# When VectorE's sequencer loads the register offsets of the chunk sums in a graph-network kernel

## The reference, cut to what matters

```python
# x [12500, 64], edge_attr_64 [400000, 64], src random, dst sorted (denser at low nodes)
msg = node_feat[src] + edge_feat
agg = jax.ops.segment_sum(msg, dst, num_segments=node_feat.shape[0])
h = jax.nn.relu(agg @ W1 + b1)
x = _layernorm(x + (h @ W2 + b2), axis=-1)
```

## Time and profile before

| | |
|---|---|
| median of three runs | 1650.94 us |
| profiled execution | 1655.22 us, span 1653.4 us |
| main stage | about 75 to 1550 us |
| busy: DVE, PE, POOL, ACT | 84%, 81%, 71%, 54% of the span |
| loads at line 898 | 125 |
| adds at line 906, marks at line 885, slots | 625, 313, 734 |

### The profile page before, as it was taken

One profiled execution on the slowest core, in us unless ns is written; L12 is line 12 of the kernel. 1 busy time (PEld: TensorE's weight loads), 2 busy tenths in 40 slices (PEclk: granted clock), 3 DMA queues, 4 the chain that ended last, 5 costly groups with the idle time before them and its releaser, 6 DMA issues. The chain is left out here.

```text
span 1653.4 us, 46879 instructions
## 1 busy us (share of the span) xinstructions
PE 1343.8 (81%) x18386; PEld 1195.7 (72%) x18387; DVE 1390.4 (84%) x2969; ACT 892.8 (54%) x1167; POOL 1169.7 (71%) x822
## 2 busy tenths in 40 slices
PE   1266777878888898888989899899988999899884
PEld 1255666767787787788878888788878887778653
DVE  5499999999988989999879898788889998788343
ACT  3734323335554554555566666566666667666352
POOL 5777888888777778778668777678677776857032
PEclk8557989999998998998999999899999999999885
DMA  6735444444444444444444444344444444433033
GB/s 178 144 82 111 104 95 106 105 104 101 102 95 91 105 89 95 101 108 90 90 97 89 96 91 92 84 86 93 97 87 90 96 91 85 83 65 69 14 70 73
DMA packets 229761, 154.81 MB, mean 94 GB/s; under 512 B 138766, under 2 KB 228478, under 8 KB 229198
## 3 DMA queue, kind: packets, MB, share of 16 engines
q1 hardware_dynamic: 126585, 124.43, 26.2%
q0 software_dynamic: 102960, 27.41, 17.0%
HBM read 146.63 MB, written 5.11 MB: 92 GB/s over the span
## 5 line engine op out<-in xcount | busy, mean ns | idle before, releaser
L611 POOL DMA_INDIRECT gmsg<-in_x,idx_t x700 | 1082.8, 1547 | 230.1 <-issue 212.7
L735 ACT CAST counts<-counted_ps 128x784 bf16<-128x784 f32 (+3 forms) x941 | 757.7, 822 | 550.9 <-PE counted_ps L1144 488.6
L1144 PE MATMUL counted_ps<-oh_key,oh_lo 128*128 128x98 bf16 (+2 forms) x5746 | 698.8, 237 | 170.6 <-DVE oh_key L941 97.5
L1161 PE MATMUL sums_ps<-x_parts,counts 128*128 128x193 bf16 (+2 forms) x5880 | 759.0, 254 | 0.6
L1144 PEld LDWEIGHTS counted_ps<-oh_key,oh_lo 128*128 128x128 bf16 x5746 | 424.8, 103 | 256.8 <-DVE oh_key L941 145.0
L1161 PEld LDWEIGHTS sums_ps<-x_parts,counts 128*128 128x128 bf16 (+2 forms) x5880 | 566.2, 121 | 8.8 <-issue 5.5
L941 DVE TENSOR_TENSOR oh_key<-chunk_ps,tables 128x1176 bf16<-128x1176 f16 (+3 forms) x734 | 542.3, 739 | 0.0
L937 DVE TENSOR_TENSOR oh_lo<-chunk_ps,tables 128x768 bf16<-128x768 f16 (+5 forms) x734 | 490.9, 669 | 32.7 <-PE counted_ps L1144 28.8
L1126 PE MATMUL chunk_ps<-onehot,cmsg 128*64 128x32 f32 (+1 forms) x4850 | 190.2, 234 | 37.3 <-DVE lists L906 24.7
L1126 PEld LDWEIGHTS chunk_ps<-onehot,cmsg 128*64 128x64 f32 x4850 | 174.4, 150 | 57.5 <-DVE lists L906 34.1
L906 DVE TENSOR_TENSOR lists<-lists,chunk_ps 64x32 f32 (+1 forms) x625 | 122.9, 197 | 94.2 <-issue 58.6
(11 more groups left out here) (102 smaller groups left out, 438.2 us busy)
## 6 DMA issues: line engine op xcount, KB each, us to landing
cmsg<-in_edge_attr SPq DMA_DIRECT2D x485, 160.0 KB
gmsg<-in_edge_attr SPq DMA_DIRECT2D x140, 160.0 KB
gmsg<-in_x,idx_t POOLq DMA_INDIRECT x700
x_parts<-in_x SPq DMA_DIRECT2D x12, 256.0 KB, 3.4
out_nodes<-x_parts SPq DMA_DIRECT2D x12, 256.0 KB, 2.6
edge_records<-counts SPq DMA_DIRECT2D x1, 1800.0 KB
lists<-in_src SPq DMA_DIRECT2D x1, 1400.0 KB
lists<-in_dst SPq DMA_DIRECT2D x1, 1400.0 KB
```

The costliest lines, as they stand in the source:

```text
L611: pool.indirect_dma_start(gmsg[:, at * D:(at + 1) * D], None, x, bass.IndirectOffsetOnAxis(ap=idx_t[:, of:of + 1], axis=0), compute_op=ALU ...
L735: nc.scalar.copy(to.rearrange("p h (m n) -> p h m n", m=m), ps.rearrange("p m (n h) -> p h m n", h=HI)).then_inc(unit_kept, 1)
L1144: mm = nc.tensor.matmul(unit_ps[u][:, col:col + slot.key_cols], oh_lo[s % RING][:, n * P:(n + 1) * P], oh_key[s % RING][:, n * slot.key_co ...
L1161: mm = nc.tensor.matmul(sums_ps[0:n, 0:XC], counts[b % 2][:, h * P:h * P + n], x_parts[:, h * XC:(h + 1) * XC], start=(h == 0), stop=(h == ...
```

## The change

The load leaves `add` and is made right after the marks of the same chunks, one visit earlier than before. Since a row of five offsets is then in use by adds still to come while the next row arrives, each kind of chunk has two sets of five registers, taken in turn. The number of loads, copies, waits, adds and marks is the same.

```diff
-            at_regs = {kind: [dve.alloc_register(f"at_{kind}{k}") for k in range(TILES)] for kind in ("gather", "count")}
+            at_regs = {kind: [[dve.alloc_register(f"at_{kind}{h}{k}") for k in range(TILES)] for h in range(2)]
+                       for kind in ("gather", "count")}
+
+            def load_offsets(quad):
+                for _, kind, i in quad:
+                    if i % TILES == 0:
+                        row = (i if kind == "count" else CCH + i) // TILES
+                        dve.load(at_regs[kind][i // TILES % 2], chunk_out[row:row + 1, 1, :])
 
             def add(place):
                 kind, i = JOB[place]
-                if i % TILES == 0:
-                    row = (i if kind == "count" else CCH + i) // TILES
-                    dve.load(at_regs[kind], chunk_out[row:row + 1, 1, :])
-                at = dve.snap(at_regs[kind][i % TILES], min_val=0, max_val=N - 1)
+                at = dve.snap(at_regs[kind][i // TILES % 2][i % TILES], min_val=0, max_val=N - 1)
...
                     for k in range(0, len(quad), 2):
                         mark(quad[k:k + 2])
+                    load_offsets(quad)
```

## The result

The changed kernel took 1623.4 us (median of four runs, 1619.5 to 1628.1) against 1651.2 us for the kernel before: ratio 0.9838, 95% interval 0.9806 to 0.9869. Taken together it is some 23 us faster.

The account below looks back on a forecast made before the run. DVE alone sets the pace up to 750 us; later neither DVE nor PE leads throughout. Terms -2 -8.5 -1, about -11 us, turn the profiled 1655.2 into 1644, and 1640 for the runs' median; range 1629 to 1653.

Parts of the forecast that it names:

- The stalls taken away: DVE's idle time before the adds, ended by "issue" or behind another add: 72.5 us less some 2, taken as 70.
- The stalls added: New DVE stalls where the slot after the marks waits for the moved load: 47 us in all.
- narrow singles: Quads with one load, both pairs 32 columns wide: 55 at 0.45 us of new stall, 25 us.
- mixed ones: Quads with one load, one pair 64 columns wide: 23 at 0.15 us of new stall, 3.5 us.
- wide ones: Quads with one load, both pairs 64 columns wide: 23, with no new stall.
- doubles: Quads with two loads: 10 at 1.5 us and 2 at 1.1 us of new stall, 17 us.
- Early part, nothing: Up to 750 us, DVE's 31.0 us removed and 31 us added cancel, so nothing is gained there.
- Of the later 25 us, I take a bit under half.: Of DVE's net saving of 25 us after 750 us, a bit under half shortens the kernel.
- Rival 1: Loads behind the marks cost nothing, as the sequencer hands on the slot meanwhile: -49 us, 1602 us; chance 0.06.
- Rival 2: PE and ScalarE hold the late part and absorb the gain: 0 +- 4, 1647 to 1655 us; chance 0.20.
- Rival 3: Load starts only once the first mark leaves the queue, some 45 us more on DVE: slower, 1675 us; chance 0.12.

Follow-up runs that it names:

- the three sets: The changed kernel, measured three times without edits against the kernel before: ratios 0.9838, 0.9881 and 0.9864.
- E13: Changed kernel with the loads between the two marks of a visit instead of after them: 1.0050 of the kernel before.
- E15: Second run of the changed kernel with loads moved behind the slots that follow the marks: 0.9679 of the kernel before.
- E3: Changed kernel without the 125 loads; row 0's offsets, loaded once, serve all sums, which land in other columns: 0.9733 of the kernel before.
- E4: Changed kernel with a visit's first load behind the slot after the marks, a second behind the next slot: 0.9686 of the kernel before, 1604 us.
- E1: Loads behind the marks only for visits of slots 0 to 314, later ones as in the kernel before: 0.9981 of that kernel.
- E2: Loads behind the marks only from the visit of slot 315 on, earlier ones as in the kernel before: 0.9880 of that kernel.
- E6: Loads behind the slots only from the visit of slot 315 on, earlier ones as in the kernel before: 0.9862 of that kernel.
- E11: Kernel before with a quarter of TensorE's products of counts and x_parts left out, late loads behind the slots: 0.9548; without the load move 0.9728.
- E7: Loads behind the slots only up to the visit of slot 314, later ones as in the kernel before: 0.9839 of that kernel.

## Why the prediction was wrong

- **The stalls taken away** (72.5 less 2, taken as 70): right, 73 to 74 by intervals in the three sets and in E13 and E15; E3 and E4 show 70 and 69.
- **The stalls added** (47 us): right, 46, and by the terms of the sum too. 55 narrow singles cost 25 us (25 forecast), 23 mixed ones 4.0 (3.5), 23 wide ones nothing, 12 doubles 17 (17).
- **Early part, nothing**: nearly. The stalls cancel to -1 us, and E1 gave 3 us.
- **The step that failed: "Of the later 25 us, I take a bit under half."** The 25 us were right (E2: 40.3 - 15.4), the share was not: 20 of 25 us came out in E2, 0.8. I read DVE's 18.5 us of waits for PE as slack that would soak up half of any saving from the first microsecond. The runs show no such even share. By amount, the first 25 us of stalls bring 20 and the next 14 bring 3 to 6 (E6, E4, E15). With PE lighter these bring 13 (E11), so they are lost to PE. By place, the saving comes out more than whole before 1200 us and hardly at all behind it. I had seen that TensorE's next products wait for the add and not for the slot, and gave that no term of its own; before 1200 us E13 gets 11 us from nothing but the change of place. Why the two stretches differ so stays open. The 23.0 us of PE waiting for DVE in the earlier trace rows lie near the 20 that came out; I named them as a bound and took half. One case can't tell whether that nearness is more than luck.
- **Size of the rest**: forecast 11, three sets 27, 20 and 22. With the share at 0.8 and E1's 3 us the sum is 23. The excess of the first set over that is within its interval. In its profile it goes with the granted clock: 0.99 and 691 us of PE in the late part, against 0.98 and 703 in the repeat. Whether the change itself raises the clock a little (0.97 before, 0.98 and 0.99 after, in the late part) stays open; E1 and E7, at 0.96 and 0.97 up to 1200 us, side with it.
- **Rival 1**, free loads behind the marks: false. The stalls are there, and E13 shows that even an instruction without a register waits for the load's end. The Trainium skill's "Advanced Engine Details and Errata", section Sequencer Loop, has other engine instructions read and queued while a control instruction executes; for this load on VectorE the trace doesn't agree (0.57 us of idle before the second mark).
- **Rival 2**, all absorbed: false for this change as a whole, but PE's part of its mechanism is what stops E6 at 23 us.
- **Rival 3**, a late start of the load: false, it starts 0.14 us before the first mark. The price of another place is seen in E13, where 85 us came in for 74 and the kernel was slower.

## What to carry to other kernels

A register load belongs where the datapath has more queued work than the load is long, and behind the last point at which the sequencer itself waits for that datapath; here that was one instruction pair further on, and worth more than the change. Where two engines wait for each other, don't take one even share of a saving: here most of the first 25 us came out and little of what went beyond, and a stall in front of work that the other engine waits for cost more than the same stall elsewhere. When a kernel's instruction list is unchanged, compare the two traces interval by interval before explaining the total, and profile the same kernel twice before trusting 1%.

## What the hardware showed that I had not expected

- The loads have two lengths, about 1.2 and 1.44 us, and in all 16 profiles with 125 loads the same 37 are the long ones. They are the loads of gather rows 97 to 115 and of the count rows loaded right after each of them, except after row 115. The cause wasn't tried.
- The same kernel's late part took 749, 763 and 758 us in three profiles with the same DVE stalls; PE's busy time there was 691, 703 and 702 us at granted clocks of 0.99, 0.98 and 0.98.
- Leaving out a quarter of the 5,880 products into `sums_ps` took 84 us from PE's busy time. A quarter of the products' own busy time of 759 us would be 190. Part of the difference can be the granted clock, which was 0.88 in that profile against 0.91; how much wasn't tried.
